# Attention: the negative maxima become a row of the second product's operand

## The chip, the cores and the metric

One core of one Trainium2 chip runs the whole program. The metric is device time in microseconds (us) of one execution.

## What is computed

The reference is two transformer layers on 4 x 512 tokens of width 512. The part that matters here is the first: attention between the layer-normed input and a context, 8 heads of 64 channels for each of 4 sequences, followed by a residual sum and a first routing step.

```python
qh = q.reshape(bs * N_HEADS, ch, T); kh = k.reshape(...); vh = v.reshape(...)
attn = jnp.einsum('bct,bcs->bts', qh * scale, kh * scale)
attn = jax.nn.softmax(attn, axis=-1)
out = jnp.einsum('bts,bcs->bct', attn, vh)
...
x = x + jnp.tanh(g_xattn[0]) * _L0_xattn_ref(_layernorm(x, axis=-1), ctx_2048, ctx_2048)
```

The three stages after it (a mixture of 8 experts, a decayed context summary with a layer norm, a mixture of 64 experts with shared experts) are touched in one semaphore only.

## The kernel before, in words

`attention` works through 16 tiles of 128 rows of x. A row tile is two heads (h = 0, 1) of 64 channels, 512 queries and 512 keys each, and softmax runs over the keys. Every engine runs its own hand-written `step(i, ...)`, software-pipelined over tiles. TensorE (PE), ScalarE (ACT) and VectorE (DVE) run two tiles per pass of a hardware loop; GpSimd (POOL) runs all its steps unrolled. Engines and DMA queues meet in counting semaphores only, each engine in its own program order.

Products with queries and keys are float32r with split operands. `k_hi` is the rounded key tile, `k_lo` the rest (POOL, `low_half`, L404). A head's 64 channels stand twice in the 128 partitions of `kd`; `q_parts` has the rounded query in one half of them and its rest in the other (ACT L681, POOL `low_query`, L418). So the product with `k_hi` gives hi*hi + hi*lo, and that with `k_lo` the two others.

Softmax needs a maximum for each query ahead of the exponential. `rough` (PE L573) computes query-major scores of the next tile, eight products `rough 0` to `rough 7`, and DVE reduces each to a negative maximum `negmax` (L734, `rough_max`). Bank `pM` is the only one for them, so a rough product waits for the reduce before it.

The scores themselves are key-major: for each of four key blocks b, `scores` (L543) puts the two big products (L549) per head into bank `pS[h]`, and then adds the negative maxima to that bank by four products of 128 columns per head (L558), whose stationary operand is one `negmax` column broadcast and whose moving operand is the bf16 identity. ACT takes the exponential (L659), and `values` (L566, float32, each product two passes) multiplies it with the context and a block of ones, so that numerator and denominator come out together in `pO`.

After block 3 of tile i-1, at the head of step i: ACT copies the denominators out (L665, L666, behind the two exponentials of block 0 of tile i), DVE takes reciprocals in three parts between its reduces (L787), POOL multiplies (L449) and adds to x (L454), DVE takes statistics of the sum (L804 to L809), POOL turns them into scale and bias (L466 to L473), and ACT writes the normed row (L691) for the router. ACT's block 3 also prepares tile i+2: `q_parts` (L681), then `k_hi` (L685), then that normed row. SyncE (SP) loads tiles, fills the DRAM tables with zeros behind them (`behind`), and at the end loads the W_out matrix (`woutT`, L361) and the context rows (`load_context`).

The tile `split_space` is declared in `build` (L102) and not used in attention; `summary`, which is `woutT` here, shares its memory.

Of the kernel before, what the change touches and what calls it, by code (L numbers as in the profile page):

```python
# [14 lines left out]
P = 128  # L15
# [4 lines left out]
HEAD = 64  # L20
# [154 lines left out]
def attention(nc, A, T):  # L175
# [6 lines left out]
    with c:  # L182
# [60 lines left out]
        parts.close()  # L243
        ctx_late = sb("ctx_late", [P, TILES - 4, D])
# [13 lines left out]
        s_full, p_ready, p_used, qk_done = sem("s_full"), sem("p_ready"), sem("p_used"), sem("qk_done")  # L258
# [46 lines left out]
        def _(sp):  # L305
# [55 lines left out]
            sp.dma_start(woutT[:], A["W_out_turned"].rearrange("(b p) d -> p b d", p=P)).then_inc(s_bias, 16)  # L361
# [4 lines left out]
            sp.wait_ge(qk_done, TILES)  # L366
# [7 lines left out]
        def _(pool):  # L374
# [47 lines left out]
            for i in range(-3, TILES + 3):  # L422
# [18 lines left out]
                if valid(i + 1):  # L441
                    low_half(i + 1, 0)
# [13 lines left out]
                if valid(i + 1):  # L456
                    low_half(i + 1, 1)
# [4 lines left out]
                if cols:  # L462
# [15 lines left out]
                    nc.gpsimd.engine_nop().then_inc(ln_done, 1)  # L478
                if valid(i + 2) and i >= 0:
                    low_query(i + 2)  # L480

        @block.tensor
        def _(pe):
# [59 lines left out]
            def scores(i, s, sb_):  # L543

                for h in range(2):

                    need(pe, p_ready, i * 8 + (sb_ * 2 + h - 1))
                    for part in (k_hi, k_lo):
                        last = nc.tensor.matmul(pS[h][:], part[:, s, h, sb_ * P:sb_ * P + P], q_parts[:, s, h, :],  # L549
                                                start=(part is k_hi), stop=False)  # L550
                if sb_ == 3:
                    last.then_inc(qk_done, 1)
                if sb_ == 0:
                    need(pe, pm_read, i * 8 + 8)
                for h in range(2):
                    for t in range(4):
                        m = h * 4 + t
                        last = nc.tensor.matmul(pS[h][:, t * P:t * P + P],  # L558
                                                negmax[:, s, m:m + 1].broadcast_to([P, P]), identb[:],
                                                start=False, stop=(t == 3))  # L560
                    last.then_inc(s_full, 1)
# [14 lines left out]
            def step(i, u, odd):  # L576
                s, o = odd, 1 - odd
                if valid(i):
                    need(pe, q_split, i + 1)
                    need(pe, k_lo_ready, i + 1)  # L580
# [63 lines left out]
        def _(act):  # L644
# [5 lines left out]
            def step(i, u, odd):  # L650
                s, o = odd, 1 - odd
                for b in range(4):
# [19 lines left out]
                    if b == 0 and valid(i - 2):  # L672
                        need(act, xnT_full, i - 1)
                        nc.scalar.copy(xnT[:].rearrange("p d t -> p (d t)"), pT[:]).then_inc(xnT_ready, 1)
                    if b == 3 and valid(i + 2):

                        need(act, qk_done, i + 1)
# [4 lines left out]
                        last.then_inc(q_hi_ready, 1)  # L682
                        need(act, kd_loaded[s], 64 * u + 128)
# [20 lines left out]
        def _(dve):  # L704
            dve.wait_ge(consts_ready, 1)
            def state_weights():
# [1273 lines left out]
def experts(nc, A, T):  # L1980
# [4 lines left out]
    with c:  # L1985
# [44 lines left out]
        rest_loaded, joined = sem("rest_loaded"), added[0]  # L2030
# [112 lines left out]
        def _(dve):  # L2143
# [34 lines left out]
            dve.wait_ge(rest_loaded, 16)  # L2178
# [98 lines left out]
```

## Time and profile before

| | us |
|---|---|
| median of 3 runs | 1113.02 (1111.92 to 1114.31) |
| the profiled execution's own time | 1115.18 |
| its span in the trace | 1113.5 |
| PE busy | 1024.4 (92%) |
| DVE busy | 722.2 (65%) |
| POOL busy | 584.8 (53%) |
| ACT busy | 500.2 (45%) |
| attention stage, first work to first table read of the next stage | 0 to 321 |

Busy time of matmuls is modelled up to their ends in a pipeline, so PE at 92% is not PE at its peak. In the attention stage PE's matmul rows follow each other almost without a hole. The clock of PE is granted in full over most of it. The later stages are unlike it, and their chains don't run through the changed lines.

### The profile page before, as it was taken

Reading aid. Unit: us, or ns where it says so; the run is one execution under the profiler, and the core shown is the slowest. Engines: PE = TensorE matmul, PEld = TensorE weight load, DVE = VectorE, ACT = ScalarE, POOL = GpSimd, SP = SyncE. Lnnn points to the kernel's source line nnn. Section 1 sums busy time; section 2 is a strip of 40 time slices with the busy share of each in tenths; the row PEclk is TensorE's granted clock in tenths of the full one; section 3 lists DMA queues with packets and bytes.
Section 4 is the critical chain, followed back from the end, with each engine's and each line's share of the span. In section 5 each row is a group of like instructions: output and inputs, shape, how many; then the busy total and the mean of one; then the engine's idle time right before and its main releaser. Section 6 shows DMA issues by size and latency. Waiting matters only on the chain. (4 is left out here: it accounts for less than half of the span.)

```text
span 1113.5 us, 18851 instructions
## 1 busy us (share of the span) xinstructions
PE 1024.4 (92%) x5364; PEld 738.3 (66%) x5364; DVE 722.2 (65%) x1704; ACT 500.2 (45%) x880; POOL 584.8 (53%) x555
## 2 busy tenths in 40 slices
PE   4999999999879999998899999999999999999960
PEld 2555555565437777775389468577778888888850
DVE  3678778777448888886688248167306666667650
ACT  3666656655238888886432211311304333333320
POOL 6566676674326667665524646356432344333551
PEclk9999999999889999999899999999999999999985
DMA  8467655577645332331540241043269999999729
GB/s 268 151 220 249 205 166 179 192 248 283 240 160 167 104 109 104 103 113 67 185 142 18 91 137 48 11 138 112 87 208 333 337 331 308 288 316 336 190 29 194
DMA packets 128254, 199.49 MB, mean 179 GB/s; under 512 B 35975, under 2 KB 44167, under 8 KB 128186
## 3 DMA queue, kind: packets, MB, share of 16 engines
q1 hardware_dynamic: 106394, 160.40, 42.6%
q0 software_dynamic: 21360, 37.48, 13.1%
q10 hardware_dynamic: 432, 0.79, 0.2%
q8 instruction: 32, 0.52, 0.2%
q14 instruction: 36, 0.29, 0.1%
HBM read 133.10 MB, written 87.56 MB: 198 GB/s over the span
## 5 line engine op out<-in xcount | busy, mean ns | idle before, releaser
L957 POOL TENSOR_TENSOR m_down_lo<-wo,m_down_hi 128x512 fp32r<-128x512 f32 x78 | 129.8, 1684 | 76.3 <-ACT m_down_hi L1053 76.3
L566 PE MATMUL bank<-win,vT 128*128 128x512 f32 x256 | 126.6, 609 | 0.0
L734 DVE TENSOR_REDUCE negmax<-bank 128x1 bf16<-128x512 f32 x128 | 85.6, 672 | 43.3 <-PE bank L573 42.9
L659 ACT ACTIVATE win<-bank 128x512 f32<-128x512 f32 x128 | 69.5, 595 | 92.3 <-PE bank L558 89.9
L1067 DVE TENSOR_TENSOR m_up_lo<-w,m_up_hi 128x1024 fp32r<-128x1024 f32 x78 | 95.5, 1226 | 12.4 <-ACT m_up_hi L1025 11.5
L2075 POOL DMA_INDIRECT out<-m_y,m_token x32 | 51.2, 1600 | 87.1 <-DMA out<-m_y,m_token 47.1
L1304 POOL DMA_INDIRECT tab<-stage_up,slot x64 | 65.6, 1025 | 53.3 <-DVE slot L1650 35.4
L2105 PE MATMUL bank<-y,m_w 128*128 128x128 f32 x736 | 89.7, 275 | 0.0
L2219 ACT ACTIVATE sh_gate_a<-bank 128x512 f32<-128x512 f32 (+1 forms) x40 | 20.5, 512 | 151.4 <-PE bank L2212 121.9
L2075 POOL DMA_INDIRECT sums<-m_y,m_token x32 | 50.6, 1581 | 71.7 <-DVE m_y L2169 41.9
L2105 PEld LDWEIGHTS bank<-y,m_w 128*128 128x128 f32 x736 | 86.4, 193 | 0.1
L573 PE MATMUL bank<-k_hi,q_parts 128*128 128x512 f32 x128 | 68.8, 548 | 16.0 <-POOL q_parts L418 13.3
L2212 PE MATMUL bank<-flat_hi,w_hi 128*128 128x512 f32 (+1 forms) x320 | 74.4, 354 | 2.5 <-DVE flat_lo L1717 1.6
L2123 PE MATMUL bank<-split_space,m_h_hi 128*128 128x512 f32 x128 | 73.7, 576 | 1.9 <-DVE split_space L2155 1.9
L2212 PE MATMUL bank<-flat_lo,w_hi 128*128 128x512 f32 (+1 forms) x320 | 72.5, 348 | 2.0 <-issue 2.0
L2212 PE MATMUL bank<-flat_hi,w_lo 128*128 128x512 f32 (+1 forms) x320 | 72.3, 348 | 0.0
L2133 ACT COPY y<-bank 128x512 f32<-128x512 f32 x64 | 37.4, 585 | 73.5 <-PE bank L2097 62.5
L981 PE MATMUL bank<-m_up_hi,m_xT_hi 128*128 128x512 f32 x156 | 68.0, 436 | 1.2 <-DVE m_up_lo L1067 1.2
L566 PEld LDWEIGHTS bank<-win,vT 128*128 128x128 f32 x256 | 48.2, 194 | 27.2 <-issue 19.5
L787 DVE RECIPROCAL attn<-attn 128x128 f32<-128x128 f32 (+1 forms) x48 | 58.5, 1220 | 7.9 <-ACT attn L666 3.9
L981 PE MATMUL bank<-m_up_lo,m_xT_hi 128*128 128x512 f32 x156 | 61.5, 394 | 0.0
L981 PE MATMUL bank<-m_up_hi,m_xT_lo 128*128 128x512 f32 x156 | 61.3, 393 | 0.0
(302 smaller groups left out, 2492.8 us busy)
## 6 DMA issues: line engine op xcount, KB each, us to landing
tab<-zeros SPq DMA_DIRECT2D x16, 1056.0 KB
m_w<-in_L_ffn_Wg SPq DMA_DIRECT2D x46, 256.0 KB
m_w<-in_L_ffn_Wu SPq DMA_DIRECT2D x46, 256.0 KB
m_w<-in_L_ffn_Wd SPq DMA_DIRECT2D x46, 256.0 KB
m_x<-tab SPq DMA_DIRECT2D x39, 256.0 KB, 2.7
ytab<-m_y SPq DMA_DIRECT2D x39, 256.0 KB, 2.0
stage_up<-tab SPq DMA_DIRECT2D x32, 264.0 KB
m_x<-tab SPq DMA_DIRECT2D x32, 264.0 KB
```

What stands on the lines that cost most here:

```text
L566: nc.tensor.matmul(pO[s * 2 + h][:], vT[:, s, sb_, h:h + 2, :].rearrange("p a c -> p (a c)"), probs[:, sb_ % 2, h, :], start=(sb_ == 0), s ...
L573: nc.tensor.matmul(rough_bank(k, m)[:], q_parts[:, s, h, t * P:t * P + P], k_hi[:, s, h, :], start=True, stop=True).then_inc(pm_full, 1)
L659: nc.scalar.activation(probs[:, b % 2, h, :], pS[h][:], ACT.Exp, scale=1.0 / HEAD).then_inc(p_ready, 1)
L734: nc.vector.tensor_reduce(negmax[:, s, m:m + 1], rough_bank(k, m)[:], AX.X, ALU.max, negate=True).then_inc(pm_read, 1)
L957: nc.gpsimd.tensor_tensor(dn_lo[:, m, :], row(wo0, e * MB + m), dn_hi[:, m, :], ALU.subtract).then_inc(dn_lo_ready, 1)
L981: last = nc.tensor.matmul(pH[s][:], x[:, s, d, :], w[:, d, :], start=(d == 0 and part == 0), stop=(d == DB - 1 and part == 2))
L1067: nc.vector.tensor_tensor(up_lo[:, at, :], blocks(w01, e * DB + half * HALF, HALF), up_hi[:, at, :], ALU.subtract).then_inc(up_lo_ready, 1)
L1304: nc.gpsimd.indirect_dma_start(T["tab1"], bass.IndirectOffsetOnAxis(slot1[:, j, k:k + 1], 0), flat[:, j, :], None, bounds_check=E1 * CAP1 ...
L2075: nc.gpsimd.indirect_dma_start(tables[e % SUMS], bass.IndirectOffsetOnAxis(token[:, e % META:e % META + 1], 0), y[:, e % RING, :], None, b ...
L2105: last = nc.tensor.matmul(pH[s][:, k * CAP1:(k + 1) * CAP1], w[:, b, :], xT[:, s, b, :], start=(b == 0), stop=(b == DB - 1))
L2123: last = nc.tensor.matmul(pY[o][:], a[:, o, :], w[:, o, :], start=(part == 0), stop=(part == 2))
L2212: last = nc.tensor.matmul(out, w[:, k, wc], x[:, d, cols], start=(d == 0 and part == 0), stop=(d == DB - 1 and part == 2))
```

## The change

The eight small products with the identity run once a tile (`maxima`, `start=True`) in place of once a key block. ACT copies each bank's result, for the 64 partitions that are not the head's, into `q_neg` (a view of `split_space`), and copies the rounded query into the other 64. `k_lo` now holds the key's rest in the head's half only; in the other half its first row is one and the others are zero, written once by DVE at the start. The product of `k_lo` with `q_neg` then gives lo*hi plus the negative maximum; lo*lo is no longer computed. POOL's work on `k_lo` is two instructions of 64 partitions, both at the end of its step, ahead of `low_query`. PE's first key block moves behind the last values products of the tile before. `woutT`, which shares memory with `q_neg`, is loaded after the last scores. Semaphore `rest_loaded` of the last stage is merged into `out_begun`.

```diff
 # SP
-            sp.dma_start(woutT[:], ...).then_inc(s_bias, 16)
             sp.wait_ge(k_lo_ready, TILES)
             load_context(0)
-            sp.wait_ge(qk_done, TILES)
+            sp.wait_ge(s_full, 8 * TILES)
+            sp.dma_start(woutT[:], ...).then_inc(s_bias, 16)
             for n in range(1, 4):
                 load_context(n)
 # POOL
-            def low_half(k, h):
+            def low_keys(k):
                 s = k % 2
                 pool.wait_ge(k_hi_ready, k + 1)
-                last = nc.gpsimd.tensor_tensor(k_lo[:, s, h, :], kd[:, s, h, :], k_hi[:, s, h, :], ALU.subtract)
-                if h:
-                    last.then_inc(k_lo_ready, 1)
+                for h in range(2):
+                    hp = slice(HEAD * h, HEAD * h + HEAD)
+                    last = nc.gpsimd.tensor_tensor(k_lo[hp, s, h, :], kd[hp, s, h, :], k_hi[hp, s, h, :], ALU.subtract)
+                last.then_inc(k_lo_ready, 1)
+                if k == 0 or not valid(k + 1):
+                    pool.drain()
...
-                if valid(i + 1):
-                    low_half(i + 1, 0)
                 if valid(i - 1):
 ...
-                if valid(i + 1):
-                    low_half(i + 1, 1)
                 if valid(i + 2) and i < 0:
                     pool.drain()
                     low_query(i + 2)
 ...
+                if valid(i + 1):
+                    low_keys(i + 1)
                 if valid(i + 2) and i >= 0:
                     low_query(i + 2)
 # PE, scores
                 for h in range(2):
-                    need(pe, p_ready, i * 8 + (sb_ * 2 + h - 1))
-                    for part in (k_hi, k_lo): ...
-                if sb_ == 0:
-                    need(pe, pm_read, i * 8 + 8)
-                for h in range(2):
-                    for t in range(4): ...
-                    last.then_inc(s_full, 1)
+                    if sb_ == 0:
+                        need(pe, neg_ready, i * 2 + (h + 1))
+                    else:
+                        need(pe, p_ready, i * 8 + (sb_ * 2 + h - 1))
+                    cols = slice(sb_ * P, sb_ * P + P)
+                    nc.tensor.matmul(pS[h][:], k_hi[:, s, h, cols], q_parts[:, s, h, :], start=True, stop=False)
+                    nc.tensor.matmul(pS[h][:], k_lo[:, s, h, cols], q_neg[:, s, h, :], start=False,
+                                     stop=True).then_inc(s_full, 1)
+            def maxima(i, s, h):
+                need(pe, p_ready, i * 8 + (h - 1))
+                need(pe, pm_read, i * 8 + (4 * h + 4))
+                for t in range(4): ...
+                last.then_inc(neg_full, 1)
 # PE, step
                 for b in range(4):
-                    if valid(i):
+                    if valid(i) and b > 0:
                         scores(i, s, b)
...
                     for h in range(2):
+                        if b == 0 and valid(i):
+                            maxima(i, s, h)
                         if b == 0 and valid(i - 1):
                             values(i - 1, o, 3, h)
+                        if b == 0 and h == 1 and valid(i):
+                            need(pe, k_lo_ready, i + 1)
+                            scores(i, s, 0)
 # ACT, step
+                    if b == 1 and valid(i + 1):
+                        need(act, s_full, i * 8)
+                        need(act, q_hi_ready, i + 2)
+                        for h in range(2):
+                            hp = slice(HEAD * h, HEAD * h + HEAD)
+                            nc.scalar.copy(q_neg[hp, o, h, :], q_parts[hp, o, h, :])
                     if b == 3 and valid(i + 2):
 ...
+                    if b == 3 and valid(i + 1):
+                        for h in range(2):
+                            other = slice(HEAD * (1 - h), HEAD * (1 - h) + HEAD)
+                            need(act, neg_full, i * 2 + (h + 3))
+                            nc.scalar.copy(q_neg[other, o, h, :], pS[h][other, :]).then_inc(neg_ready, 1)
+                    if b == 3 and valid(i + 2):
 ...
 # DVE, once, ahead of its first step
+            for h in range(2):
+                other = slice(HEAD * (1 - h), HEAD * (1 - h) + HEAD)
+                nc.vector.tensor_copy(k_lo[other, :, h, :], zeros[other, 0:D].unsqueeze(1).broadcast_to([HEAD, 2, D]))
+            dve.drain()
+            for h in range(2):
+                first = slice(HEAD * (1 - h), HEAD * (1 - h) + 1)
+                nc.vector.tensor_copy(k_lo[first, :, h, :], onesb[first, 0:1].unsqueeze(2).broadcast_to([1, 2, D]))
 # DVE, rough_max
-                    need(dve, s_full, k * 8 - 8)
+                    need(dve, neg_full, k * 2 - 2)
```

## Rows read from the trace of the kernel before

**Rows 1.** Busy time by stretch: PE, PEld, DVE, ACT, POOL (instructions), granted clock, DMA share.

```profile
150.00:200.00 50.00, 49.57 (x257) 29.82 (x257) 39.27 (x95) 30.31 (x54) 35.64 (x45) 1.00 0.62 196
```

**Rows 2.** Groups of instructions, 100 to 250 us, PE: busy us, mean ns.

```profile
L566 PE MATMUL bank<-win,vT 128*128 128x512 f32 x142 | 68.6, 595 | 0.0
...
L558 PE MATMUL bank<-identb,negmax 128*128 128x128 bf16 x288 | 22.3, 220 | 0.0
```

**Rows 3.** Who waited for whom, 100 to 250 us: total us, times, longest.

```profile
ACT win L659 <- PE bank L558: 47.5, 28, 3.4
POOL tab L427 <- DVE slot L768: 24.7, 9, 3.0
```

**Rows 4.** Timeline of ACT, the first denominator copy of tiles 0, 1, 13, 14, 15.

```profile
37.48 0.58 ACT L665 COPY attn<-bank 64x512 f32<-64x512 f32 x1 [0.85 <-PE bank L566]
...
52.92 0.58 ACT L665 COPY attn<-bank 64x512 f32<-64x512 f32 x1 [0.91 <-PE bank L566]
...
255.12 0.58 ACT L665 COPY attn<-bank 64x512 f32<-64x512 f32 x1 [0.91 <-PE bank L566]
...
273.52 0.58 ACT L665 COPY attn<-bank 64x512 f32<-64x512 f32 x1 [0.91 <-PE bank L566]
...
294.55 0.58 ACT L665 COPY attn<-bank 64x512 f32<-64x512 f32 x1 [6.92 <-PE bank L566]
```

**Rows 5.** Groups of instructions, 100 to 250 us, POOL and ACT.

```profile
L408 POOL TENSOR_TENSOR k_lo<-wout,k_hi 128x512 fp32r<-128x512 f32 x18 | 23.2, 1286 | 0.0
...
L691 ACT ACTIVATE xn<-x_sb,ln 128x512 f32 x9 | 7.3, 814 | 0.0
...
L665 ACT COPY attn<-bank 64x512 f32<-64x512 f32 x9 | 5.2, 582 | 8.7 <-PE bank L566 8.7
```

**Rows 6.** Timeline of one step and the start of the next (start us, us).

```profile
150.48 0.49 PE L549 MATMUL bank<-q_parts,k_hi 128*128 128x512 f32 x1 [0.18 <-issue]
...
151.94 1.08 ACT L659 ACTIVATE win<-bank 128x512 f32<-128x512 f32 x2 [0.44 <-PE bank L558]
...
155.80 1.75 DVE L787 RECIPROCAL attn<-attn 128x256 f32<-128x256 f32 x1
...
164.91 0.69 DVE L734 TENSOR_REDUCE negmax<-bank 128x1 bf16<-128x512 f32 x1 [0.26 <-PE bank L573]
...
166.10 0.26 POOL L473 TENSOR_SCALAR ln<-mv,rstd 128x1 f32<-128x1 f32 x1
...
166.78 1.14 ACT L685 CAST k_hi<-wout 128x512 fp32r<-128x512 f32 x2
...
167.29 0.40 PE L549 MATMUL bank<-q_parts,k_hi 128*128 128x512 f32 x1
```

**Rows 7.** Timeline of the start of the stage.

```profile
4.46 0.29 POOL L399 CAST identb<-ident 128x128 bf16<-128x128 f32 x1
...
5.76 0.69 DVE L795 BATCH_NORM_STATS2 bn<-x_sb 128x6 f32<-128x512 f32 x1 [5.64 <-DMA x_sb<-in_x]
...
15.36 1.25 ACT L681 CAST q_parts<-q 64x512 fp32r<-64x512 f32 x2 [3.77 <-POOL q L439]
...
17.97 2.60 POOL L418 TENSOR_TENSOR q_parts<-q,q_parts 64x512 fp32r<-64x512 f32 x2 [0.16 <-issue]
...
20.61 1.08 ACT L659 ACTIVATE win<-bank 128x512 f32<-128x512 f32 x2 [2.84 <-PE bank L558]
```

**Rows 8.** Groups of instructions, whole span, DVE.

```profile
L1067 DVE TENSOR_TENSOR m_up_lo<-w,m_up_hi 128x1024 fp32r<-128x1024 f32 x78 | 95.5, 1226 | 12.4 <-ACT m_up_hi L1025 11.5
...
L2151 DVE CAST m_h_hi<-m_gh 128x128 fp32r<-128x128 f32 x64 | 15.5, 242 | 4.7
```

**Rows 9.** Timeline of POOL near the end of the stage.

```profile
282.99 1.29 POOL L454 TENSOR_TENSOR x_sb<-x_sb,attn 128x512 f32<-128x512 f32 x1 [3.25 <-issue]
```

**Rows 10.** Busy time by stretch, columns as in Rows 1.

```profile
265.00:270.00 5.00, 3.19 (x16) 1.52 (x14) 2.57 (x7) 1.90 (x3) 3.49 (x5) 1.00 1.05 397
...
285.00:290.00 5.00, 2.69 (x5) 1.60 (x6) 2.47 (x21) 1.12 (x2) 1.01 (x3) 0.68 0.93 312
```

More of the change, by code:

```diff
@@ L243, in attention @@
         parts.close()
+        q_neg = T["split_space"][:].rearrange("p (s h d) -> p s h d", s=2, h=2)
         ctx_late = sb("ctx_late", [P, TILES - 4, D])
@@ L257, in attention @@
         s_bias = sem("summary_bias_loaded")
-        s_full, p_ready, p_used, qk_done = sem("s_full"), sem("p_ready"), sem("p_used"), sem("qk_done")
+        s_full, p_ready, p_used = sem("s_full"), sem("p_ready"), sem("p_used")
+        neg_full, neg_ready = sem("neg_full"), sem("neg_ready")
         sums_ready, po_read, x1_ready = sem("sums_ready"), sem("po_read"), sem("x1_ready")
@@ L359, in load_context @@
                     sp.dma_start(ctx_at[t], c_v[:, t, :]).then_inc(ctx_loaded[n], 16)
-            sp.dma_start(woutT[:], A["W_out_turned"].rearrange("(b p) d -> p b d", p=P)).then_inc(s_bias, 16)
             sp.dma_start(bin_col[:], A["L1_xattn_b_in"].rearrange("(b p) -> p b", p=P),
@@ L365, in _ @@
             load_context(0)
-            sp.wait_ge(qk_done, TILES)
+            sp.wait_ge(s_full, 8 * TILES)
+            sp.dma_start(woutT[:], A["W_out_turned"].rearrange("(b p) d -> p b d", p=P)).then_inc(s_bias, 16)
             for n in range(1, 4):
@@ L545, in scores @@
                 for h in range(2):
-                    need(pe, p_ready, i * 8 + (sb_ * 2 + h - 1))
[L548 to L552, printed above, removed]
-                if sb_ == 0:
-                    need(pe, pm_read, i * 8 + 8)
-                for h in range(2):
[L556 to L560, printed above, removed]
-                    last.then_inc(s_full, 1)
+                    if sb_ == 0:
[9 more added lines that the diff above has]
+                need(pe, pm_read, i * 8 + (4 * h + 4))
+                for t in range(4):
+                    m = h * 4 + t
+                    last = nc.tensor.matmul(pS[h][:, t * P:t * P + P], negmax[:, s, m:m + 1].broadcast_to([P, P]), identb[:],
+                                            start=True, stop=True)
+                last.then_inc(neg_full, 1)
             def values(k, s, sb_, h):
@@ L674, in step @@
                         nc.scalar.copy(xnT[:].rearrange("p d t -> p (d t)"), pT[:]).then_inc(xnT_ready, 1)
+                    if b == 1 and valid(i + 1):
[4 more added lines that the diff above has]
+                            nc.scalar.copy(q_neg[hp, o, h, :], q_parts[hp, o, h, :])
                     if b == 3 and valid(i + 2):
-                        need(act, qk_done, i + 1)
+                        need(act, s_full, i * 8 + 8)
                         need(act, q_ready, i + 3)
@@ L2029, in experts @@
         rest = T["summary"]
-        rest_loaded, joined = sem("rest_loaded"), added[0]
+        rest_loaded, joined = T["out_begun"], added[0]
         block = c.enter_context(nc.Block(no_gpsimd_drain=True))
@@ L2177, in _ @@
                                             ALU.mult).then_inc(back_read, 1)
-            dve.wait_ge(rest_loaded, 16)
+            dve.wait_ge(rest_loaded, 16 * B + 16)
             nc.vector.tensor_tensor(rest[:], rest[:], x_sb[:, TILES - TPB:, :], ALU.add).then_inc(back_read, 1)
```

1 line of the change is left out of this document (removed).

## The prediction

> **What bounds the kernel now.** I read first the busy time by stretch, then the groups of instructions, the waits and the timeline of the attention stage; the change touches nothing on the chains of the others. In attention PE is busy 49.6 of 50 us at full clock, and DVE, the next, 39.3 [rows 1]. ACT waits 47.5 us in 150 for the small products that end each score block, and POOL has a rest of some 2.7 us a tile before its scatter [rows 3]. So PE's order of work sets the pace, and the others have slack. The first denominator copy marks the pace: from tile 1 to tile 13 it goes from 52.92 to 255.12, 16.85 us a tile [rows 4].
>
> **What the change removes.** A group of eight small products takes PE 0.43 us in its order: the 288 rows of [rows 2] are nine tiles of 32, and between the last big product before such a group and the next product after it the timeline leaves that much, eight times some 0.054; the mean of 220 ns is pipeline depth. Three groups of four go: 1.3 us a tile, 21 us over 16 tiles. If PE's order stayed the bound, the period would be 15.55 us. That is the gain to be had.
>
> **What it adds on PE: nothing in products, but an order.** `maxima`, values, `maxima`, values, then the first score block. Call S the time at which PE is through with rough product 7 and starts the step. Before, the first exponentials ran at about S + 1.5 (151.94 against 150.48) [rows 6], because PE did the block 0 scores first. Now they need more.
>
> **What it adds on ACT.** Four copies of 64x512 a tile: two from PSUM, nearest row 0.58 each [rows 5], and two from SBUF, nearest two in 1.25 [rows 7], 2.4 us together. ACT has that time (30.3 busy of 50, [rows 1]), and the SBUF pair in block 1 lies in its old wait [rows 3]. What counts is the PSUM pair's place: in program order between the query cast and the key cast, and the second of them waits for the second `maxima`. The key cast, the normed row, the block 0 exponentials and the denominator copies are all queued behind it. From S: maxima 0.23, one values product 0.86 (two passes), maxima 0.22, and 0.2 to the end of the pipeline and the semaphore make 1.5; the copy 0.58; two key casts 1.14 [rows 6]; the normed row 0.75 net of overlap (0.81, [rows 5]); two exponentials 1.08 [rows 6]; two denominator copies 1.16 [rows 5]. DVE can take its first reciprocal at S + 6.2.
>
> **The second leg.** From that reciprocal the way to the next step is already a chain in the trace: reciprocals between reduces, POOL's products and sum, statistics, reduces 5 to 7, each a turn with a rough product on the one bank. Before, it goes from 155.80 to 167.29, 11.49 us [rows 6]. PE's absence from the waits in it (reduce 5 waited 0.26 for PE, [rows 6]) can take off 0.3, so 11.2. The two legs close a loop: 6.2 + 11.2 = 17.4 us a tile, whatever PE has to do. In the kernel before, the first leg was 155.80 - 150.48 = 5.3, and there DVE itself (place, reduce 0), not ACT, was the last to be ready. With part of a loop turn that shows on PE every second tile (the 150.48 start), I take **17.5 us** against 16.85: bounds 17.2 (all of it overlapped) and 17.8 (a timetable of all four engines drawn up from these durations).
>
> **POOL.** The two subtractions keep their price though they have half the partitions: `low_query`, with 64 partitions, takes 2.60 for two [rows 7], `low_half` with 128 takes 1.29 each [rows 5]. They lose their cover, which was POOL's waits for reciprocals. The last scale and bias end at 166.36 [rows 6], 0.9 before the step; 0.6 with the shorter leg. So `k_lo` is ready at S + 2.1, just before the first score block wants it (S + 2.2), `low_query` ends at S + 4.7, and rough product 0, which was done at S + 3.3 before, follows it: PE waits over 1 us. Reduce 0 then ends at S + 5.9, and the reciprocal could start at S + 6.0. This hides behind ACT's 6.2 by 0.2 us only: moving the ACT copies alone wouldn't bring the loss back. If both were gone, DVE's own order would be next.
>
> **The start of the stage.** DVE writes `k_lo`'s constant half ahead of its first statistics: four copies of 1024 elements. A 1024-element operation of two operands takes 1.23, a 128-element cast 0.24 [rows 8]; between these ends, nearer to the first by its size, I take 0.9 each, 3.6 in all, bounds 1.0 and 4.9. They begin when the constants are ready at 4.8, some 0.9 before x lands at 5.7 [rows 7], so 2.7 us late (0 to 4). The Trainium skill ("VectorE: DVE Perf Modes", Mode 2x_2P) lets a single-source fp32 copy in SBUF run at two elements a clock; by that rule the four would take 2.8 us by my estimate, and the delay would be 1.9. No row here shows such a long copy.
> Then `k_lo` of tile 0 now comes behind `low_query(1)`, which can start at 16.6 when the cast of 15.36 ends, and takes 2.6 [rows 7]; 1.1 for scale and bias and 2.55 for `low_keys` lead to 22.9. The first exponential comes at 24.0 with PE still at low clock, against 20.61 [rows 7]: 3.4 us. Nothing later makes up for either, since the loop above is the pace. Together +6.1.
>
> **The tiles.** From tile 0 to 1 it was 15.44 [rows 4], then 12 intervals of 16.85, then 18.40. With 17.5: +2.1, +7.8, and for the last, which has a stretch of saturated DMA [rows 10] in it, +0.9 (0 if that delay is absorbed, +1.9 if it adds in full). +10.8.
>
> **The last tile and SP.** From tile 14 to 15 it was 21.03 [rows 4]. POOL's sum at 282.99 was 3.25 us late for no engine [rows 9], while the DMA engines were full, as at 265 [rows 10]; DVE, then PE behind `turned_column`, waited for it, and PE's clock fell to 0.68 [rows 10]. `woutT`, 1 MB, now isn't in that stretch. If the late issue goes with it, ACT's later start still makes PE wait some 1.6 us, and I get 16.4: up to -4.6; or nothing changes. No row decides, so I take the middle, -2.3. The later `woutT` puts 1 MB ahead of the context rows (2.7 us at the 370 GB/s of that stretch), which have some 6 us until PE reads them; bin_col and the merged semaphore cost nothing: the first is still loaded early, the second waits for the same transfer.
>
> **Sum**: 6.1 + 10.8 - 2.3 = +14.6 us. The profiled execution would go from 1115.18 to 1129.8; the median shown lies 2.16 below that execution, so I predict 1113.02 + 14.6 = **1127.6**. The case's own range is the bounds added in part: head 4 to 8, tiles 6 to 16, tail -4.6 to 0, so 1119 to 1136.
>
> **Rivals.**
> *A. The loop doesn't close and PE stays the bound.* The denominator copies would have to come no later than before. For it: PE is 99% busy [rows 1] and 1.3 us less is sure. Against: ACT is in program order. The period would be 15.6, near DVE's own occupancy of 14.0 (16.85 less its waits). 14 intervals of -1.3 with the head's +6.1: 1101. Half a gain, 16.2, still ends at 1110.
> *B. The pauses cost PE its clock.* PE would wait about 1 us for rough 0 and again in reduces 5 to 7 of each tile. Where it was idle nearly 3 us of a stretch and the clock fell to 0.68, values products took twice the time; where it was idle 1.8 of 5 us, the clock stayed at 1.00 [rows 10]. I expect the latter. If in every tile 3 us of PE's work ran at 1.2 GHz and half of that showed, 1.5 x 14 = 21 more: 1149. The Trainium skill ("TensorE: Matmul & The Clock Gate", Part 1) has the clock fall to half when PE idles and return with activity; the trace agrees at 285 to 290, and gives no case against the change below a pause of 1.8 us.
> *C. A draw.* The loop takes 17.0 (tiles +3), the head's copies hide (+3.4) and the tail gives its full 4.6: +1.8, 1114.8.
> *D. The change doesn't do what it says:* the counts in the code leave no room for it.
>
> **How the numbers follow.** Forecast 0.75, A 0.12, B 0.07, C 0.06. The range 1111 to 1137 leaves out most of A below and B above. Within 0.2% is within 2.2 us, about what a measurement can tell: only C and the edge of A, 0.04. Faster 0.13, slower 0.83.
>
> **What would show it.** In the changed trace: L558's successor 8 a tile; the first denominator copy every 17.5 us, waiting for nothing on PE but late behind the exponentials, which wait for ACT's own queue; DVE's reciprocal waiting for the copy; rough 0 waiting for POOL's `low_query`; the first statistics at 8.5; the first exponential near 27; the clock at 1.00 between 50 and 250. A copy interval under 16.8 makes the prediction wrong at its main step; one over 18.5 with a clock under 1.00 means rival B.

## The result, and the profile after

The changed kernel takes 1155.14 us (median of four runs, 1153.03 to 1157.83) where the kernel before takes 1112.79: 1.0377 times as long, 95% interval 1.0358 to 1.0396. That is 42 us slower. The sign is the predicted one, the size is not: 14.6 us were forecast, and 1155 lies above the stated 1111 to 1137. The profiled execution has a span of 1153.9 us against 1113.5, so there are 40.4 us to find in the trace.

**Where they are.** The first lines are the head of the page of the kernel after (share of the span and count of instructions for each engine).

```profile
span 1153.9 us, 18203 instructions
...
PE 1023.5 (89%) x4980; PEld 727.8 (63%) x4980; DVE 749.9 (65%) x1708; ACT 536.8 (47%) x944; POOL 586.2 (51%) x555
```

PE runs 384 products fewer than before, as it should, and is busy no less: its remaining products take longer. The busy time by stretch (columns as in [rows 1]) says where:

```profile
150.00:200.00 50.00, 38.80 (x148) 21.35 (x149) 38.35 (x83) 30.09 (x53) 30.81 (x39) 0.97 0.55 180
200.00:250.00 50.00, 44.08 (x163) 25.94 (x162) 38.66 (x81) 31.61 (x56) 29.83 (x36) 0.93 0.48 156
```

Against [rows 1], PE has fallen from 49.6 busy in 50 us to between 38.8 and 44.1, and its clock from 1.00 to 0.93 and 0.97. No other engine is full. So the bound is a chain, as forecast. The first denominator copies of tiles 0, 1, 14 and 15 give the pace; this is the timeline of ACT in the kernel after, to be read against [rows 4]:

```profile
43.65 0.58 ACT L675 COPY attn<-bank 64x512 f32<-64x512 f32 x1
...
61.05 0.58 ACT L675 COPY attn<-bank 64x512 f32<-64x512 f32 x1
...
297.36 0.58 ACT L675 COPY attn<-bank 64x512 f32<-64x512 f32 x1
...
318.18 0.58 ACT L675 COPY attn<-bank 64x512 f32<-64x512 f32 x1
```

Tile 0 comes 6.2 us later than before, tile 1 again 2.0. From tile 1 to tile 13 it is 236.3 us against 202.2: **34.1 us more, where 7.8 were forecast**. From 13 to 14 it is 2.4 more, from 14 to 15 (332.78) 6.4 less, and the rest of the span takes 2.2 more, which I have not followed. The intervals between tiles are uneven: 17.4, 17.1, 18.8, 22.8, 17.8, 21.0, 19.5, 21.1, 18.7, 22.4, 17.7, 22.2, 17.1, 20.8, 14.6. Five of them are 17.1 to 17.8, near the 17.5 of the forecast, but they are not undisturbed turns of its loop: PE's steps themselves (from one first `maxima` to the next, between 113 and 253 us) are 18.0 to 22.1 apart. In these steps the first leg, from the step's start S to the first reciprocal, takes 7.1 to 7.6 (once 6.5) against the forecast's 6.2, and the second leg 11.5 to 15.0 against 11.2. Two things lengthen them.

**First: DVE's small operations stand still.** This is the timeline of one step in the kernel after (start us, duration; PE's next step began at 153.54):

```profile
152.99 2.59 POOL L412 TENSOR_TENSOR k_lo<-wout,k_hi 64x512 fp32r<-64x512 f32 x2 [0.17 <-issue]
...
154.68 0.92 DVE L778 COPY top<-m 128x2 f32 x1
...
155.65 2.60 POOL L423 TENSOR_TENSOR q_parts<-q,q_parts 64x512 fp32r<-64x512 f32 x2
155.68 1.28 DVE L780 CAST idxf<-i 128x2 f32<-128x2 uint32 x1
...
157.04 1.38 DVE L783 TENSOR_SCALAR onehot<-iota_e,idxf 128x8 f32<-128x8 f32 x2
...
158.57 0.58 ACT L675 COPY attn<-bank 64x512 f32<-64x512 f32 x1
158.72 0.10 PEld L542 LDWEIGHTS bank<-mask,before 128*128 128x128 bf16 x1 [2.24 <-DVE mask L785]
158.72 0.18 PE L542 MATMUL bank<-mask,before 128*128 128x8 bf16 x1 [1.80 <-DVE mask L785]
...
160.78 1.75 DVE L818 RECIPROCAL attn<-attn 128x256 f32<-128x256 f32 x1
```

A copy of two elements a partition takes 0.92, a cast of two 1.28, two scalar operations 1.38 together. The ends tell why: 155.60, 156.96 and 158.42 lie 0.01 to 0.2 behind the ends of POOL's second, third and fourth subtraction (155.58, 156.95, 158.25, each two of equal length). Where POOL is silent, at the last tile, the same three lines are short:

```profile
315.17 0.15 DVE L778 COPY top<-m 128x2 f32<-128x2 f32 x1
315.39 0.17 DVE L780 CAST idxf<-i 128x2 f32<-128x2 uint32 x1
315.64 0.36 DVE L783 TENSOR_SCALAR onehot<-iota_e,idxf 128x8 f32<-128x8 f32 x2
```

So the mask comes some 2.9 us later than these durations would have it, PE, in order, waits 1.8 with rough product 0 queued behind the positions (the two small products of L542 and L543), and the reciprocal starts at 160.78, S + 7.2 instead of the forecast's S + 6.2. ACT's second copy had ended at 159.74, in time. The Trainium skill ("SBUF — State Buffer", SBUF: two separate sides) says that GpSimd and those VectorE operations that use the second port pair take turns by an exclusive lock, held for a whole instruction; the ends above agree with it.

**Second: POOL's x sum is late for no engine.** Timeline of another step of the kernel after:

```profile
135.01 0.94 SPq L297 DMA_DIRECT2D vT<-in_ctx_by_column  x2
...
137.55 0.59 ACT L675 COPY attn<-bank 64x512 f32<-64x512 f32 x1
...
139.03 1.08 POOL L432 DMA_INDIRECT tab<-xn,slot  x1 [2.09 <-DVE slot L799]
139.13 0.99 SPq L334 DMA_DIRECT2D w<-in_L_ffn_wi  x2
...
148.30 1.27 POOL L457 TENSOR_TENSOR x_sb<-x_sb,attn 128x512 f32<-128x512 f32 x1 [2.98 <-issue]
...
149.82 0.69 DVE L835 BATCH_NORM_STATS2 bn<-x_sb 128x6 f32 x1 [3.11 <-POOL x_sb L457]
...
151.91 0.50 PE L579 MATMUL bank<-k_hi,q_parts 128*128 128x512 f32 x1 [3.02 <-DVE negmax L765]
```

Ahead of the sum stands a drain. The scatter of this step (the indirect DMA of L432) starts at 139.03 and SP's bulk transfers at 139.13, and the DMA share is 0.80 to 1.07 in the stretches read from 141 to 154. The same places in the kernel before, first [rows 6]'s step, then the one of tile 13:

```profile
153.93 0.94 SPq L295 DMA_DIRECT2D vT<-in_ctx_by_column  x2
...
155.26 1.07 POOL L427 DMA_INDIRECT tab<-xn,slot  x1 [2.96 <-DVE slot L768]
...
158.25 0.94 SPq L332 DMA_DIRECT2D w<-in_L_ffn_wi  x2
...
161.86 1.27 POOL L454 TENSOR_TENSOR x_sb<-x_sb,attn 128x512 f32<-128x512 f32 x1 [0.32 <-issue]
...
256.22 0.95 SPq L332 DMA_DIRECT2D w<-in_L_ffn_wi  x2
256.28 1.08 POOL L427 DMA_INDIRECT tab<-xn,slot  x1 [2.48 <-DVE slot L768]
...
265.24 1.27 POOL L454 TENSOR_TENSOR x_sb<-x_sb,attn 128x512 f32<-128x512 f32 x1 [2.79 <-issue]
```

Where the scatter came 3.0 us ahead of the bulk transfers, the sum was 0.32 late; where both started together, 2.79. A wait of 0.3 or a little more is there in most tiles of both kernels. Long waits, over 2 us, were two before (6.0 us, tiles 13 and 14, [rows 9]); now they are six, in every second tile (2.2 to 3.3 each, 16.3 us).

Both partners moved. From the step's start S (150.48 before, 132.53 here) the scatter goes from S + 4.8 to S + 6.5, since its slots come behind the late mask. The bulk transfers go from S + 7.8 to S + 6.6: in SP's program order they stand behind the loads of keys and `vT`, and the load of `vT` waits for the last values products of the tile just finished, which PE's new order puts ahead of the block 0 scores. So that load starts 2.5 us ahead of ACT's first denominator copy (135.01 and 137.55), where it started 0.06 ahead before (153.93 and 153.99).

Behind the late sum DVE's statistics (3.11) and PE (3.02, through the reduces) wait too.

**Then PE's clock falls.** Busy time, columns as in [rows 1]:

```profile
160.00:162.00 2.00, 2.00 (x6) 1.20 (x5) 1.91 (x2) 1.97 (x4) 1.49 (x2) 0.63 0.44 144
```

At 161.33 four values products take 3.18 us, 0.8 each, against 0.5 at full clock. Between 100 and 250 us the clock falls to its lower level (0.50, 1.2 GHz) four times, for some 4 us each. Two of the falls follow a pause of PE behind the late sum (2.81 us ending at 111.5, 2.28 ending at 232.3), two, this one among them, a pause behind the late mask (1.80 ending at 158.7, 1.62 ending at 217.9).

**The start.** The four constant copies of the kernel after, and the first statistics:

```profile
4.93 1.39 DVE L731 CAST k_lo<-zeros 64x1024 fp32r<-64x1024 f32 x2 [4.81 <-POOLq L403]
6.40 1.38 DVE L735 CAST k_lo<-onesb 1x1024 fp32r<-1x1024 bf16 x2
7.70 0.67 DVE L826 BATCH_NORM_STATS2 bn<-x_sb 128x6 f32<-128x512 f32 x1
```

They take 0.7 each, not 0.9, and the statistics are 1.9 us late, not 2.7. The Trainium skill ("VectorE: DVE Perf Modes", Mode 2x_2P) had given just this 1.9; measurement and rule agree.

### The profile page after: what moved, and what is told of

The parts are those of the page before. It is cut to its first block and busy times, and to the rows that moved or that the text cites. A ratio compares the mean times of both kernels' runs of the same rounds, so it can differ in the third digit from the quotient of the medians.

```text
span 1153.9 us, 18203 instructions
## 1 busy us (share of the span) xinstructions
PE 1023.5 (89%) x4980; PEld 727.8 (63%) x4980; DVE 749.9 (65%) x1708; ACT 536.8 (47%) x944; POOL 586.2 (51%) x555
## 5 line engine op out<-in xcount | busy, mean ns | idle before, releaser
L572 PE MATMUL bank<-win,vT 128*128 128x512 f32 x256 | 134.0, 629 | 0.0
L579 PE MATMUL bank<-k_hi,q_parts 128*128 128x512 f32 x128 | 72.1, 575 | 40.5 <-DVE negmax L765 22.0
L2250 ACT ACTIVATE sh_gate_a<-bank 128x512 f32<-128x512 f32 (+1 forms) x40 | 20.5, 514 | 151.3 <-PE bank L2243 122.5
L579 PEld LDWEIGHTS bank<-k_hi,q_parts 128*128 128x128 f32 x128 | 26.2, 206 | 90.5 <-DVE negmax L765 65.6
L555 PE MATMUL bank<-q_parts,k_hi 128*128 128x512 f32 x128 | 59.8, 467 | 2.6 <-POOL k_lo L412 2.6
## 6 DMA issues: line engine op xcount, KB each, us to landing
tab<-zeros SPq DMA_DIRECT2D x16, 1056.0 KB, 10.9
```

The lines of the kernel that those rows point to most:

```text
L572: nc.tensor.matmul(pO[s * 2 + h][:], vT[:, s, sb_, h:h + 2, :].rearrange("p a c -> p (a c)"), probs[:, sb_ % 2, h, :], start=(sb_ == 0), s ...
L579: nc.tensor.matmul(rough_bank(k, m)[:], q_parts[:, s, h, t * P:t * P + P], k_hi[:, s, h, :], start=True, stop=True).then_inc(pm_full, 1)
```

## The experiments

Each ratio is to the kernel before on the same chip, with its 95% interval. "Pace" is the mean interval from tile 1 to tile 13 in the profiled execution.

```
kernel             us       ratio  interval          pace   first copy
before           1112.79   1                         16.85    37.5
after            1155.14   1.0377  1.0358 to 1.0396  19.69    43.7
bulk_late        1154.54   1.0319  1.0271 to 1.0367  19.36    43.9
khi_first        1159.14   1.0368  1.0334 to 1.0402  19.62    43.6
before_keys_late 1161.03   1.0374  1.0329 to 1.0419  19.97    43.0
sem_for_drain    1138.77   1.0195  1.0157 to 1.0232  18.58    43.4
half_with_drain  1135.53   1.0249  1.0227 to 1.0271  18.55    41.8
half_keys        1121.39   1.0064  1.0047 to 1.0082  17.40    41.3
small_ops        1123.04   1.0092  1.0056 to 1.0128  17.43    42.5
half_khi         1112.45   1.0036  1.0025 to 1.0046  17.21    42.0
half_khi_small   1112.04   0.9980  0.9960 to 0.9999  16.66    42.4
before_sem       1105.16   0.9926  0.9906 to 0.9947  16.82    36.4
before_sem_small 1101.70   0.9937  0.9912 to 0.9961  16.81    35.9
```

The level moved by some 0.5% between sets of runs (the kernel before had medians of 1108 to 1116), so the ratios are to be compared, not the times.

**bulk_late** keeps SP's bulk transfers back until the exponentials have freed a block:

```
                     if n == 0:
+                        sp.wait_ge(p_ready, u * 16 - 8)
                         behind(u)
```

> The kernel after, with SP's weight loads and table zeroing (behind) held back until the exponentials of key block 3 of tile 2u-2 (one wait on p_ready). Theory: in every second tile GpSimd's sum into x stands still for 2.2 to 3.3 us until the scattered rows of the tile have landed, and they land late because the bulk transfers start with them. Then the six long intervals (20.8 to 22.8 us) between denominator copies fall to some 18, as the others are, the idle time ahead of the x sum falls from 18.5 us in total to under 6, and the run takes 15 to 24 us less: 1131 to 1140 us. Rival (the sum is late for another reason, such as instruction fetch, which has nothing to do with these transfers): the long intervals stay, 1150 to 1160 us.

It missed. The intervals of 21 to 23 us are gone but for one of 22.4, yet the pace is 19.36, and the x sum still sits idle for 15.9 us against 18.5, now over 1 us in seven tiles (1.3 to 3.1). Most of these are other tiles than before: with the bulk transfers later other scatters meet them. The ratio is 0.6 points lower, with intervals that just overlap. Where the transfers lie in time was not a clean handle, so the next run takes away the wait that they lengthen.

**sem_for_drain** orders the x sum behind the two products by a semaphore that they raise, not by a drain:

```
                         last = nc.gpsimd.tensor_tensor(attn[:, cols_], attn[:, cols_], numer[:, cols_], ALU.mult)
+                        if i < TILES:
+                            last.then_inc(attn_done, 1)
...
-                        pool.drain()
+                        pool.wait_ge(attn_done, 2 * i)
                         nc.gpsimd.tensor_tensor(x_sb[:, i - 1, :], x_sb[:, i - 1, :], attn[:],
```

> The kernel after, where GpSimd waits ahead of its sum into x for a semaphore of the two products before it, and not with a drain; the transfers are as they were. Theory A (the drain itself waits for the scatter's own transfers): the 2 to 3 us ahead of the x sum vanish although the bulk transfers stay, so 12 to 24 us less, 1131 to 1143 us. Theory B (GpSimd can't start any compute instruction, or can't fetch, while its scatter is held up): no change at that row, 1150 to 1160 us.

From 1.0377 to 1.0195, about 20 us. The data that the sum needs are as old as before; only what the drain waited for besides is gone. In the groups of 100 to 250 us of sem_for_drain (busy, mean ns | idle before) 0.6 us of idle time is left, where the kernel after has 12.1:

```profile
L460 POOL TENSOR_TENSOR x_sb<-x_sb,attn 128x512 f32<-128x512 f32 x8 | 10.1, 1268 | 0.6
```

So POOL's drain had been waiting for more than the two products. What POOL has under way there besides is its scatter; when a scatter lands the trace doesn't show, so that the drain waits for the landing is the likeliest reading, not a measured one. The waits of the same kernel now show the mask in its place:

```profile
PE bank L545 <- DVE mask L788: 14.3, 8, 1.8
```

The clock falls here too, in every second step, though the sum is never late. One such fall:

```profile
153.00:157.00 4.00, 4.00 (x12) 2.89 (x12) 3.56 (x9) 2.78 (x6) 2.66 (x3) 0.57 0.46 166
```

It follows a pause of 1.83 us behind the mask that ended at 152.5. In the four steps with a fall the second leg takes 11.9 to 12.0 us, in the same kind of step of half_keys, below, in which no fall occurs, 11.2. So some 0.7 us in every second tile go with the fall.

**khi_first** puts ACT's key casts ahead of the copies of the negative maxima. That takes 1.1 us off the leg that the prediction named as the last.

```
                         last.then_inc(q_hi_ready, 1)
+                        need(act, kd_loaded[s], 64 * u + 128)
+                        for h in range(2):
+                            last = nc.scalar.copy(k_hi[:, s, h, :], kd[:, s, h, :])
+                        last.then_inc(k_hi_ready, 1)
                     if b == 3 and valid(i + 1):
...
-                    if b == 3 and valid(i + 2):
-                        (the same casts)
```

> The kernel after, with ScalarE's two key casts ahead of the two copies of the maxima (they fill the wait of about 4 us that ScalarE has there). Forecast's theory (ScalarE's queue between maxima and exponentials is the leg that sets the period): 1.1 us a tile less, 15 us in all, 1140 us. Rival (VectorE, late with the mask and reduce 0 behind GpSimd, starts its reciprocal only after the copy is there): 5 us less at most, 1150 to 1156 us.

1.0368 against 1.0377: nothing (1159.14 us is above both ranges, in a set of runs in which the kernel before took 1115.81). In the kernel after, ACT's leg isn't the last.

**before_keys_late** leaves everything in the kernel before but POOL's order: both key subtractions run at the end, ahead of `low_query`, with a drain between.

```
-                if valid(i + 1):
-                    low_half(i + 1, 0)
...
-                if valid(i + 1):
-                    low_half(i + 1, 1)
...
+                if valid(i + 1):
+                    low_half(i + 1, 0)
+                    low_half(i + 1, 1)
+                    pool.drain()
                 if valid(i + 2) and i >= 0:
                     low_query(i + 2)
```

> The kernel before, with one part of the change alone: both subtractions for k_lo at the end of GpSimd's step, ahead of low_query (whole 128 partitions, one drain between them and low_query). Theory (the order on GpSimd is what costs: VectorE's small copies stand still behind 5 us of GpSimd work in place of 2.6, the mask, rough product 0 and the scatter come later, and the scatter falls among the bulk transfers): some 2 us a tile and more in every second one, 25 to 45 us slower, 1138 to 1158 us. Rival (ScalarE's and TensorE's new order cost the time, GpSimd's is hidden): under 10 us slower, below 1123 us.

1.0374: POOL's order alone costs as much as the whole change. Two lines of its groups (100 to 250 us), two of its waits, and the x sum of one step in its timeline:

```profile
L408 POOL TENSOR_TENSOR k_lo<-wout,k_hi 128x512 fp32r<-128x512 f32 x14 | 17.5, 1268 | 1.2 <-issue 1.2
...
L752 DVE TENSOR_SCALAR onehot<-iota_e,idxf 128x8 f32<-128x8 f32 x14 | 8.8, 670 | 0.5
```

```profile
DVE rows L760 <- PE bank L540: 20.9, 8, 2.6
...
PE bank L549 <- POOL k_lo L408: 12.9, 7, 1.9
```

```profile
148.93 1.27 POOL L452 TENSOR_TENSOR x_sb<-x_sb,attn 128x512 f32<-128x512 f32 x1 [0.32 <-issue]
```

L752 takes 670 ns where the kernel before has 228: the small operations are held here too. It isn't a copy of the loss, though, and the second half of its theory missed. The scatter doesn't fall among the bulk transfers: it starts at 142.32 in this step, they at 145.33, 3.0 us apart as in the kernel before, and the sum is late by more than 0.5 us only in the last two tiles. The intervals are even, 20.2 to 20.5 in tiles 3 to 12. The cost comes in other ways: PE here wants `k_lo` at the very start of a step and waits 12.9 us for it, there is one drain more, and the mean clock from 100 to 250 us is 0.92. It shows that the order can cost 42 us, not that it costs them in the same way. With PE's old order the bulk transfers stay behind the scatter, which fits the reading that it is PE's new order that brings them forward; no run changed PE's order alone.

**half_keys** is sem_for_drain with head 0's subtraction back behind the query row, only head 1's at the end:

```
+                if valid(i + 1):
+                    low_keys(i + 1, 0)
                 if valid(i - 1):
                     pool.wait_ge(po_read, i)
...
                 if valid(i + 1):
-                    low_keys(i + 1)
+                    low_keys(i + 1, 1)
```

> sem_for_drain, and of the two subtractions for k_lo that of head 0 goes back to its place behind the query row (where GpSimd waits anyway), so that one of 1.3 us, not two, stands ahead of low_query. Theory (the GpSimd work at the end of its step is the cost, by VectorE's small copies standing still behind it and by the late low_query): 0.8 to 1.3 us a tile less than sem_for_drain (1.0195 of before), 12 to 20 us, so 1.002 to 1.009 of before. Rival (what is left of the loss is ScalarE's and TensorE's order): 1.017 or more.

1.0064, as its theory had it, and the pace is 17.40, with PE's clock at 1.00. Here the forecast's loop can be measured: over nine steps the first leg takes 6.2 to 6.5 us and the second 10.9 to 11.3, for a forecast of 6.2 and 11.2.

**small_ops** keeps sem_for_drain's order of POOL, and writes the two small copies of `choose` as reductions over an axis of one:

```
-                nc.vector.tensor_copy(row(T["top0"], k), m8[:, 0:2])
+                nc.vector.tensor_reduce(row(T["top0"], k), m8[:, 0:2].unsqueeze(2), AX.X, ALU.max)
...
-                nc.vector.tensor_copy(idxf[:], i8[:, 0:2])
+                nc.vector.tensor_reduce(idxf[:], i8[:, 0:2].unsqueeze(2), AX.X, ALU.max)
```

> sem_for_drain, and two of VectorE's small copies in choose (top0 of 2 elements, idxf of 2 elements) are done by a reduce over an axis of one element, which gives the same values. Measures what holds them. Theory A (copies and casts in SBUF, unlike reduces, stand still while GpSimd runs a two-input operation): they take under 0.2 us each in place of 1.0 and 1.3, the one-hot operation behind them still takes up to 1.4, the mask comes 1 to 2 us earlier, and the run takes 8 to 16 us less than sem_for_drain, 1.006 to 1.013 of before. Theory B (VectorE's write to these tiles or the address of the loop is slow): the reduces take as long as the copies did, 1.018 to 1.021.

1.0092, inside the range of theory A, pace 17.43. Its timeline, with POOL busy throughout:

```profile
158.77 2.59 POOL L413 TENSOR_TENSOR k_lo<-wout,k_hi 64x512 fp32r<-64x512 f32 x2 [0.18 <-issue]
...
160.18 0.15 DVE L781 TENSOR_REDUCE top<-m 128x2 f32 x1
160.42 0.15 DVE L783 TENSOR_REDUCE idxf<-i 128x2 f32<-128x2 uint32 x1
160.65 0.88 DVE L786 TENSOR_SCALAR onehot<-iota_e,idxf 128x8 f32<-128x8 f32 x2
161.44 2.60 POOL L424 TENSOR_TENSOR q_parts<-q,q_parts 64x512 fp32r<-64x512 f32 x2
161.60 1.15 DVE L788 TENSOR_TENSOR mask<-onehot 128x8 bf16<-128x8 f32 x1
...
163.13 0.94 DVE L795 TENSOR_TENSOR chosen<-chosen,mask 128x8 bf16<-128x8 bf16 x1
```

The same values, moved by a reduction, pass beside POOL's subtraction in 0.15 each; scalar operations and operations of two inputs are still held. That settles the first mechanism: it is the kind of DVE operation that meets POOL, not DVE's load. Two ways of bringing the mask forward, half_keys and small_ops, end on the same 17.4.

**half_with_drain** is half_keys with the drain back.

> half_keys, but with POOL's drain back ahead of the x sum in place of the semaphore. If the two mechanisms add, the drain costs here what it cost in the kernel after (1155 to 1139, 16 us): 1133 to 1140 us. Rival: the drain was only late because POOL's two subtractions had pushed the scatter into the bulk transfers; with one subtraction back in place the mask and the scatter come earlier and the drain costs little but for tiles 13 and 14 (9 us in the kernel before): 1122 to 1131 us.

1.0249 against half_keys' 1.0064: the drain costs 20 us here as in the kernel after. The rival, that it hurts only because two subtractions had pushed the scatter into the bulk transfers, missed. One line of its groups, 100 to 250 us, and one of its steps in the timeline:

```profile
L462 POOL TENSOR_TENSOR x_sb<-x_sb,attn 128x512 f32<-128x512 f32 x8 | 10.2, 1274 | 10.2 <-issue 10.2
```

```profile
170.37 1.07 POOL L433 DMA_INDIRECT tab<-xn,slot  x1 [2.36 <-DVE slot L804]
...
171.38 1.14 SPq L335 DMA_DIRECT2D w<-in_L_ffn_wi  x2
...
178.84 1.28 POOL L462 TENSOR_TENSOR x_sb<-x_sb,attn 128x512 f32<-128x512 f32 x1 [2.08 <-issue]
```

The step starts at 164.79, so the scatter is back at S + 5.6, but the bulk transfers are still at S + 6.6, 1.0 us behind it, and the sum is 2.1 late. The first leg of this step is 6.2 us as forecast, so a mask that is 1 us late is not needed for the stall.

**half_khi and half_khi_small** add khi_first to half_keys, the second also the reductions of small_ops.

> half_keys with ACT's k_hi casts ahead of the copies of the negative maxima; the small copies stay copies. Theory of the forecast's loop, once POOL and DVE are out of its way: the casts' 1.3 us leave ACT's leg, some 0.7 to 1.1 us a tile: 1105 to 1114 us. Rival: the small copies still hold the mask, and the gain of half_khi_small came mostly from them: 1116 to 1122 us.

> half_keys, small_ops and khi_first together (the key casts ahead of the copies of the maxima). Once GpSimd and VectorE are out of the way, the forecast's loop through ScalarE (6.2 + 11.2 us) should be the pace, and khi_first shortens that by 1.1: 16.3 to 16.6 us a tile against 16.85 before, with the start 6 us later and the end 6 us shorter. Theory: 0.990 to 1.000 of before. Rival (VectorE's own work and GpSimd's low_query still set the pace at 17 us or more): 1.003 to 1.010.

half_khi comes to 1.0036, a pace of 17.21, by ratio inside its rival's range and by its median inside the theory's. The pace decides: the casts' 1.1 us brought 0.2 a tile, not 0.7. With the reductions as well the pace is 16.66, just above the 16.3 to 16.6 expected, and the ratio 0.998. At 17.4 two ways to the reciprocal end almost together, ACT's and the one from the mask through rough 0. In half_keys the reciprocal starts 1.2 to 1.4 us behind ACT's first copy, so as the second ends or just behind it; in half_khi it starts up to 2.4 behind, so ACT is no longer the last. Neither edit alone shortens the loop by much, both do: the first leg of half_khi_small is 5.4 to 5.8 us.

**before_sem and before_sem_small** put the semaphore, then also the reductions, into the kernel before.

> The kernel before, with GpSimd's drain ahead of its sum into x replaced by a wait for its two products' semaphore, as in sem_for_drain. Theory (the drain waits for the scatter's transfers, and the two late sums of the kernel before, 2.79 us at 265 and 3.25 us at 283, are that): both vanish, and with the second TensorE's 3 us pause and its time at half clock near 290; 5 to 10 us faster, 1104 to 1110 us. Rival (the context loads or the last tile's own chain set that end anyway): within 2 us of no change.

> The kernel before with the semaphore in place of POOL's drain and the two small DVE copies of `choose` written as reductions. Theory: the copies stand still only while POOL subtracts; in the kernel before this was one copy of 1.06 us, but PE is the bound there and does other products meanwhile, so nothing or little comes of it: 1101 to 1106 us, ratio 0.989 to 0.994. Rival: the mask was late for PE in the kernel before too, and each tile gains up to 0.9 us: 1091 to 1099 us.

before_sem takes 0.9926 of the kernel before. Its sums of tiles 13 and 14, idle 2.79 and 3.25 before [rows 9], in its timeline of POOL:

```profile
261.04 1.27 POOL L457 TENSOR_TENSOR x_sb<-x_sb,attn 128x512 f32<-128x512 f32 x1
...
276.47 1.28 POOL L457 TENSOR_TENSOR x_sb<-x_sb,attn 128x512 f32<-128x512 f32 x1
```

The last two intervals become 16.5 and 15.4, from 18.4 and 21.0. The reductions add nothing that can be measured (0.9937, intervals overlapping): in the kernel before one copy a tile was held for 1.05 us, but PE had other products to do. These two are the fastest of the kernels here, and the semaphore has nothing to do with the change studied.

**Put together**, in points of the ratio: the drain costs 1.8 in the changed kernel and 0.7 in the one before, so the change brings 1.1, or 12 us. The place of head 0's subtraction is 1.3 (sem_for_drain to half_keys), 15 us. The loop of 17.4 is 0.8 (half_keys to half_khi_small), 9 us. What is left between half_khi_small and before_sem is 0.5, 6 us, the size of the head: their first copies lie 42.4 - 36.4 = 6.0 apart. By tile 15 it is 3.7, so the rest of the 6 comes later, and I have not followed it. That 12 + 15 + 9 + 6 = 42 is no check, since the terms are steps of one chain of ratios. The steps were taken in one order only; another order may share the middle two differently, since small_ops also gave 1.0 alone. Each ratio is good to 0.1 to 0.5 points.

## Why the prediction was wrong in size

**What bounds before, what is removed:** right. PE's order set the pace, and three of four groups are gone. Their time came back as PE's waits.

**The loop.** The structure was right: PE stops being the bound, two legs close a loop, and 17.5 us a tile was forecast. half_keys and small_ops measure a pace of 17.4, and half_keys both legs as forecast. As a forecast for the kernel as changed it failed, and in two steps.

The first step that failed is the **POOL** paragraph: "They lose their cover, which was POOL's waits for reciprocals." It priced the move by what POOL's own queue does, `k_lo` at S + 2.1 and `low_query` to S + 4.7, both right within half a microsecond (2.0 and 4.7). It left out what POOL's 5.2 us in a row do to DVE's place and choose, which the kernel before showed in small: [rows 6]'s step has a two-element copy of 1.06 us (151.28 to 152.34) that ends with POOL's second subtraction (152.30), which the paragraph doesn't name. So the reciprocal came at S + 7.1 to 7.6 in nearly all steps, not 6.2, and the mask, not ACT, held it. This is the "hides behind ACT's 6.2 by 0.2 us only" of that paragraph, turned over: the way through DVE and PE was the longer one by 1 us. On khi_first, which moved ACT's leg, the forecast's reasoning missed outright.

The second is **the second leg's 11.2**, taken from one step of the kernel before in which the sum wasn't late. It was 11.5 to 15.0. The late sum was seen in [rows 9] and put down to full DMA engines at the tail; but the drain that ties the sum to the scatter wasn't named, so its return in every second tile wasn't costed. The paragraph on PE, "nothing in products, but an order", followed that order to ACT's exponentials only. It also lets SP's loads and the bulk transfers behind them start 1.2 us sooner in the step, while the scatter starts 1.7 later, so they meet. half_with_drain shows the stall with the scatter 1.0 us ahead of the transfers, before_keys_late shows none at 3.0. The drain's price is 12 us beyond what it cost before.

**The clock, rival B:** in part. Pauses up to 1.0 us left the clock at 1.00, as expected (half_keys, in which PE is busy 45 to 46 of 50 us). But the prediction leaned on a stretch of [rows 10] in which 1.8 us idle had left the clock at 1.00, and pauses of that length did not stay harmless: the clock fell behind waits for the mask of 1.6 to 1.8 us, in the kernel after and, without any late sum, in sem_for_drain (though not behind each of them), and also behind the waits of 2.3 to 2.8 that the drain caused. B gave 1149, with 3 us of work at the lower clock in every tile; in sem_for_drain it is a fall in every second tile, with some 0.7 us each. For the kernel after itself pauses and clock weren't separated.

**The head** is right in sum, 6.2 for 6.1, wrong in terms: the copies cost 1.9, not 2.7, the order of POOL and ACT 4.2, not 3.4. The expected 24.0 + 2.7 for the first exponential was 26.56.

**The tail:** 6.4 us less, for a forecast of 2.3 and a bound of 4.6. The interval 14 to 15 is 14.6, and POOL's sum in it is idle 0.32, not 3.25. That `woutT`, now elsewhere, is the reason is likely but not tested. The interval before kept its stall (3.29) and grew by 2.4, where 0.9 had been forecast. So 5.6 of the 21.0 had been the stall with its clock, since before_sem gets 15.4 without moving `woutT`.

**Rivals A and C** are excluded for the kernel as changed: its pace is 19.69, theirs were 15.6 and 17.0. half_khi_small, at a pace of 16.66, is as near as A comes: even with its three repairs PE's saving isn't cashed beyond 0.2 us a tile.

## What to carry to other kernels

When work is moved on one engine, list what every other engine does in its new place and look for those operations' long forms in the trace: a tiny operation that takes seven times its usual time in one spot, and ends with another engine's instruction, is being held by it, and it tells what will happen when the spot gets wider. Follow a new order on one engine also into the DMA queues that wait for it. Order a single dependence by a semaphore on the instruction that produces it, not by a drain, where the same engine has indirect transfers under way. When a forecast rests on one leg being 0.2 us longer than the next, treat the shorter one as uncosted work and go through it instruction by instruction.

## What the runs showed of the hardware

- A small DVE copy, cast or scalar operation in SBUF that meets a two-input operation of POOL waits until that instruction of POOL ends: 0.15 to 0.18 us alone, 0.92 and 1.28 beside it (copy, cast), 1.38 for two scalar operations in a row. A reduction of the same data took 0.15 beside it. DVE operations with two SBUF inputs were held too (0.94 and 1.15 against 0.15 and 0.17). The Trainium skill ("GPSIMD Engine Reference", Specifications) names the two-input operations among those that contend; these rows agree.
- A drain on POOL behind indirect scatters took up to 3.3 us with nothing else to wait for, and the wait was gone when a semaphore took its place, in both kernels. It was long where bulk transfers started within 1.0 us of the scatter, 0.3 where they came 3.0 behind, and in bulk_late 1.3 to 2.9 where they had begun 9 us before it. That it waits for the scatter to land is inferred.
- A subtraction of 64x512 on POOL costs 1.27, one of 128x512 1.27 to 1.29: halving the partitions halves nothing.
- PE's clock stayed at 1.00 with pauses up to 1.0 us in every step (half_keys), and fell to 0.50 for some 4 us behind pauses of 1.6 to 2.8 us (after) and of 1.7 to 1.8 (sem_for_drain, in every second step).
